# Scan stage and last two stages of a four-layer kernel: one program per engine, chunks overlapped, blocks in fixed slots

## The reference, cut to what matters

```python
# stage 4: gated linear scan over all 2048 tokens; its input is a layernorm, then an RMS norm
xn = x / max(norm(x), 1e-12) * sqrt(128) * gamma
q, kv, a = split(xn @ W_qkva.T); a = sigmoid(a)
h[t] = a[t] * h[t-1] + kv[t]                    # per feature
out = q * h
# stages 7 and 8: dense feed-forward, 128 -> 512 -> 128 (the first with its own layernorm gain and shift)
x = x + relu(x2 @ w1 + b1) @ w2 + b2
x = x + relu(layernorm(x) @ W1 + b1) @ W2 + b2
```

## Time and profile before

| | |
|---|---|
| three runs | 942.45, 938.83, 939.75 us; median 939.75 |
| profiled execution | 939.33 us, span 937.5 us |
| TensorE busy | 749.5 us, 80% of the span |
| VectorE busy | 694.7 us, 74% |
| ScalarE busy | 553.9 us, 59% |
| GpSimd busy | 429.6 us, 46% |
| mean granted TensorE clock | 0.891 of full speed |

### The profile page before, as it was taken

The page is one execution under the profiler, slowest core; times in us unless marked ns, Lnnn a source line. Parts: engine busy times, 40 slices in busy tenths (PEclk is TensorE's granted clock), DMA queues, the critical chain, the costliest instruction groups (busy, mean ns, idle before and its releaser), DMA issues. The chain is left out here.

```text
span 937.5 us, 10990 instructions
## 1 busy us (share of the span) xinstructions
PE 749.5 (80%) x3306; PEld 474.2 (51%) x3306; DVE 694.7 (74%) x1644; ACT 553.9 (59%) x877; POOL 429.6 (46%) x463
## 2 busy tenths in 40 slices
PE   4788996898988799886579888868677867767776
PEld 3566763454655577764456665633232222224554
DVE  6686875989896377776766667778888778784675
ACT  5254664746745356543136666768799887784333
POOL 6547655454442045556426766624433123303554
PEclk9998999979877689999769999978899888898799
DMA  4100000001000000001000000000000000000001
GB/s 137 58 12 15 23 15 25 23 16 31 23 8 11 1 1 1 0 1 34 1 0 1 1 1 0 1 0 1 1 1 0 1 1 0 1 1 0 1 0 46
DMA packets 9610, 11.59 MB, mean 12 GB/s; under 512 B 720, under 2 KB 5712, under 8 KB 9552
## 3 DMA queue, kind: packets, MB, share of 16 engines
q1 hardware_dynamic: 9552, 10.89, 4.0%
HBM read 9.84 MB, written 1.05 MB: 12 GB/s over the span
## 5 line engine op out<-in xcount | busy, mean ns | idle before, releaser
L949 POOL TENSOR_TENSOR rbuf<-B,rbuf 128x512 fp32r<-128x512 f32 x154 | 200.6, 1305 | 175.6 <-ACT rbuf L872 111.2
L917 DVE TENSOR_TENSOR B<-B,spread_bank 128x512 f32<-128x512 f32 x128 | 87.1, 682 | 45.2 <-ACT B L864 35.2
L872 ACT ACTIVATE rbuf<-B 128x512 fp32r<-128x512 f32 x132 | 82.9, 628 | 41.5 <-PE y_bank L697 32.4
L695 PE MATMUL y_bank<-rbuf,WH 128*128 128x512 f32 x174 | 75.5, 434 | 29.8 <-POOL rbuf L949 18.8
L864 ACT ACTIVATE B<-gate_banks,WR 128x512 f32<-128x512 f32 x96 | 66.0, 688 | 39.1 <-PE gate_banks L697 29.0
L904 DVE TENSOR_TENSOR B<-B,up_banks 128x512 f32<-128x512 f32 x68 | 46.5, 684 | 49.0 <-PE up_banks L697 30.1
L861 ACT ACTIVATE B<-gate_banks 128x512 f32<-128x512 f32 x68 | 40.8, 599 | 64.6 <-PE gate_banks L697 63.5
L695 PE MATMUL gate_banks<-XH,WH 128*128 128x512 f32 x168 | 75.5, 450 | 2.5 <-ACT YT L1273 0.8
L477 POOL TENSOR_SCALAR small<-small 128x4 f32<-128x4 f32 x36 | 7.5, 209 | 141.0 <-DVE small L378 140.4
L697 PE MATMUL y_bank<-rbuf,WL 128*128 128x512 f32 x174 | 70.2, 404 | 0.0
L696 PE MATMUL y_bank<-rbuf,WH 128*128 128x512 f32 x174 | 70.2, 404 | 0.0
(11 more groups left out here) (290 smaller groups left out, 2060.3 us busy)
## 6 DMA issues: line engine op xcount, KB each, us to landing
STG<-in_w_split SPq DMA_DIRECT2D x27, 256.0 KB, 2.7
X<-in_x SPq DMA_DIRECT2D x4, 256.0 KB, 6.0
out<-X SPq DMA_DIRECT2D x4, 256.0 KB, 2.3
WR<-in_w_raw SPq DMA_DIRECT2D x1, 524.5 KB, 5.5
STG<-in_w_exact SPq DMA_DIRECT2D x2, 256.0 KB, 2.7
STG<-in_w_split SPq DMA_DIRECT2D x5, 64.0 KB, 1.9
STG<-in_w_split SPq DMA_DIRECT2D x1, 192.0 KB, 2.3
STG<-in_w_split SPq DMA_DIRECT2D x1, 128.0 KB, 2.1
```

The costliest lines, as they stand in the source:

```text
L695: nc.tensor.matmul(dst, w[0], x[0], start=start, stop=False)
L872: nc.scalar.activation(rbuf[n % 2][:, :], HO[n % 3], ACT.Copy).then_inc(hh_ready, 1)
L917: nc.vector.tensor_tensor(HO[n % 3], src, SP[:, :], ALU.mult).then_inc(h_ready, 1)
L949: e_.tensor_tensor(rbuf[2 + n % 2][:, :], AO[n % 2] if f.dense else HO[n % 3], rbuf[n % 2][:, :].bitcast(F32), ALU.subtract).then_inc(hl_r ...
```

## The change

- The scan stage is played once, when chunk 0 is reached, as one written-out list per engine (`gated_pe`, `gated_act`, `gated_dve`, `gated_pool`), with two sets of SIG, HS and YS. The carry is read from the other HS. Chunk 0's products stand on TensorE in expert stage 3, ahead of its last two down projections; its sigmoid stands on ScalarE ahead of that stage's result copy, behind a one-element sigmoid that brings the table.
- Three fronts (stage 4 chunks 2 and 3, stage 5 chunk 0; ON_ACT) are normalised on ScalarE, with a scale and a bias from GpSimd, turned into bank R in place of TN, and XH comes from ScalarE too.
- Stage 4's norm takes one power of 128 x variance in place of two.
- The last group of weight pieces may no longer be done in the scan stage, only from expert stage 5 on.
- Expert stages 1 and 5 project block 1 ahead of the first routing weights.
- The dense stages become eight slots of four blocks with four buffers of each kind (`ring_*`). ScalarE writes both the high part and the relu from the bank; the subtraction is on VectorE, and for the fourth block of slots 0 to 5 on GpSimd; the down projection lags three blocks. A slot ends with one front and one tail. The first two projections stand in the last step of stage 6.

```diff
+        ON_ACT = ((4, 2), (4, 3), (5, 0))
+        def norm_bank(n, c):
+            return R if count(n, c) >= count(7, 2) or (n, c) in ON_ACT else TN
...
+                if n == 4:
+                    chain(nc.gpsimd.tensor_scalar(ve[:, :], mv[:, :, 1], float(P), 1e-24 * EPS, ALU.mult, ALU.max))
...
+            if pos == 1 and on_act:
+                a.wait_ge(rstd_ready, m + 1)
+                a.wait_ge(norm_turned, m)
+                for j in range(TL):
+                    i = nc.scalar.activation(XN[:, j, :], X[:, c * TL + j, :], ACT.Identity, scale=rs[:, j:j + 1],
+                                             bias=nb[:, j:j + 1])
...
                 for at_ in lagged(f, c, b, f.lag):
                     down(*at_)
+                    if f is FFN1 and at_ == (NC - 1, f.blocks - 3):
+                        scan_pe(pe, 0)
...
+            if c >= 2:
+                a.wait_ge(yt_ready, count(4, c - 1))
             a.wait_ge(scan_in, 3 * c + 1)
-            nc.scalar.activation(buf[c % 2], SB[c % 2][0][:, :], ACT.Sigmoid).then_inc(sig_ready, 1)
+            nc.scalar.activation(SIG[c % 2], SB[c % 2][0][:, :], ACT.Sigmoid).then_inc(sig_ready, 1)
...
+        def gated_pe(pe):
+            tail_pe(pe, 3, 3)
+            scan_pe(pe, 1)
+            tail_pe(pe, 4, 0)
+            front_pe(pe, 4, 2, 2)
+            scan_pe(pe, 2)
+            front_pe(pe, 4, 3, 2)
+            tail_pe(pe, 4, 1)
+            front_pe(pe, 5, 0, 2)
+            scan_pe(pe, 3)
+            tail_pe(pe, 4, 2)
+            front_pe(pe, 5, 0, 4)
+        def gated_act(a):
+            scan_act(a, 1)
+            front_act(a, None, 4, 2, 1)
+            front_act(a, None, 4, 2, 2)
+            front_act(a, None, 4, 3, 1)
+            scan_act(a, 2)
+            front_act(a, None, 4, 3, 2)
+            front_act(a, None, 5, 0, 1)
+            front_act(a, None, 5, 0, 2)
+            scan_act(a, 3)
+            nc.scalar.activation(junk[:, 1:2], zero, ACT.Exp)
+            front_act(a, None, 5, 0, 6)
+        def gated_dve(v, chain):
+            front_dve(v, chain, 4, 2, 0)
+            scan_dve(v, chain, 0)
+            scan_out(v, 0)
+            tail_dve(v, chain, 3, 3)
+            front_dve(v, chain, 4, 3, 0)
+            tail_dve(v, chain, 4, 0)
+            scan_dve(v, chain, 1)
+            front_dve(v, chain, 4, 2, 3)
+            scan_out(v, 1)
+            front_dve(v, chain, 5, 0, 0)
+            scan_dve(v, chain, 2)
+            tail_dve(v, chain, 4, 1)
+            front_dve(v, chain, 4, 3, 3)
+            scan_out(v, 2)
+            front_dve(v, chain, 5, 1, 0)
+            front_dve(v, chain, 5, 0, 3)
+            scan_dve(v, chain, 3)
+            front_dve(v, chain, 5, 0, 5)
+            tail_dve(v, chain, 4, 2)
+            scan_out(v, 3)
+            for pos in (7, 8, 9):
+                front_dve(v, chain, 5, 0, pos)
+            front_dve(v, chain, 5, 1, 1)
...
+        def ring_pe(pe, j):
+            for b in range(RB4):
+                k = RB4 * j + b
+                if k >= 2:
+                    ring_up(pe, k)
+                if k == 3:
+                    project_pe(pe, NC - 1)
+                if k >= 3:
+                    ring_down(pe, k - 3)
+            if ring_front(j):
+                front_pe(pe, *ring_front(j), 2)
+            tail_pe(pe, *ring_tail(j))
...
+        def ring_act(a, j):
...
+            for b in range(RB4):
...
+                nc.scalar.activation(HID[n % DEEP], UPD[n % DEEP][:, :], ACT.Relu, bias=bias).then_inc(hh_ready, 1)
...
+                nc.scalar.activation(AOD[n % DEEP], UPD[n % DEEP][:, :], ACT.Relu, bias=bias).then_inc(act_done, 1)
+                if b == 0 and j:
+                    if ring_front(j - 1):
+                        front_act(a, None, *ring_front(j - 1), 2)
+                if b == 2:
+                    if j:
+                        result(j - 1)
...
+        def ring_dve(v, chain, j):
+            front, last = ring_front(j), ring_front(j - 1) if j else None
+            for b in range(RB4):
+                if not ring_low_on_pool(RB4 * j + b):
+                    ring_low(nc.vector, v, RB4 * j + b)
+                if b == 0 and front:
+                    front_dve(v, chain, *front, 0)
+                if b == 1:
+                    if last:
+                        front_dve(v, chain, *last, 3)
+                    if front:
+                        front_dve(v, chain, *front, 1)
+            tail_dve(v, chain, *ring_tail(j))
...
-                limit = {"stage0": 0, FFN0: 1, "attn": 2, FFN1: 2, "scan": 3, FFN2: 3}.get(body, 3)
+                limit = {"stage0": 0, FFN0: 1, "attn": 2, FFN1: 2, "scan": 2, FFN2: 3}.get(body, 3)
```

More of the change, by code:

```diff
@@ L1433, in build, with gated_pool @@
+        def gated_pool(g, chain):
+            for n, c in ((4, 2), (4, 3), (5, 0), (5, 1)):
+                front_pool(g, chain, n, c, 0)
         UL = 16
@@ new lines, in ring_tail, with ring_low_on_pool, ring_up @@
+        def ring_tail(j):
+            return divmod(count(6, NC - 1) + j, NC)
+        def ring_low_on_pool(k):
+            return k % RB4 == 3 and k // RB4 < SLOTS - 2
+        def ring_up(pe, k):
+            j, b = divmod(k, RB4)
+            f, c = ring_of(j)
+            n = FFN3.block0 + k
+            if b == 0:
+                pe.wait_ge(piece_ready, READY_AT[f.up])
+                pe.wait_ge(piece_ready, READY_AT[f.down])
+                pe.wait_ge(xl_ready, count(f.norm, c) + 1)
+            if k < DEEP:
+                pe.wait_ge(r_ready, PALL - 1 + k // 2)
+            else:
+                pe.wait_ge(act_done, n - DEEP + 1)
+            mm3(UPD[n % DEEP][:, :], wh(f.up, b * P), (chunk(XH, c, PAD), chunk(XL, c, PAD)), True, True)\
+                .then_inc(first_full, 1)
@@ new lines, in ring_down @@
+        def ring_down(pe, k):
+            j, b = divmod(k, RB4)
+            f, c = ring_of(j)
+            n = FFN3.block0 + k
+            if b == 0:
+                if j == 0:
+                    pe.wait_ge(oq_read, NC - 1)
+                else:
+                    pe.wait_ge(yt_ready, count(f.tail, c) - (1 if j > 1 else 0))
+            pe.wait_ge(hl_ready, n + 1)
+            mm3(YD[j % 2][:, :], wh(f.down, b * P), (HID[n % DEEP], LOD[n % DEEP]), b == 0, b == RB4 - 1)\
+                .then_inc(down_done, 1)
@@ L1796, in build @@
         HOOKED = ("attn", "keys", "queries")
+        RINGS = ("ring3", "ring4")
         def walk(which, eng, chain, do_front, do_tail):
-            late = False
             for body, c, tail, norm, route in slots():
-                was_late, late = late, body == "scan" or isinstance(body, Ffn) and body.dense
-                late_norm = norm if not late else route if was_late else None
+                if body in RINGS:
+                    j = c + NC * RINGS.index(body)
+                    ring_dve(eng, chain, j) if which == 2 else (ring_pe, ring_act)[which](eng, j)
+                    continue
+                if body == "scan":
+                    if c == 0:
+                        gated_dve(eng, chain) if which == 2 else (gated_pe, gated_act)[which](eng)
+                    continue
                 def hook(pos):
@@ L1818, in hook @@
                     else:
[L1819 removed]
+                        front = norm if pos in NORM_STEPS else route
                         if front:
@@ L1824, in walk @@
                 else:
-                    first = () if body != "scan" else (3, 0) if which == 2 else (2,)
-                    for pos in first:
-                        hook(pos)
                     args = [c, hook]
@@ L1901, in _ @@
                     attn_pool(g, chain, c, hook, lambda: work(limit))
+                elif body == "scan":
+                    if c == 0:
+                        gated_pool(g, chain)
                 else:
```

225 lines of the change are left out of this document (152 added, 73 removed), and 1 row of the table STEPS_AT.

## The result

The changed kernel takes 899.8 us (median of 4 runs, 897.5 to 900.9) against 939.3 for the kernel before on the same chip: ratio 0.958, 95% interval 0.956 to 0.960. The prediction was 907, in 8 of 10 cases 896 to 922. So it was faster as forecast, and by 7 us more than forecast. The profiled execution took 897.48 us for a span of 895.7; against the profiled one of before that is 41.8 us less.

What follows compares the result with a forecast made beforehand. TensorE bounds the expert stage, no engine the serial scan stage; the last two stages lie between. Terms -15.5 - 3 - 1 + 4 - 17 = -32.5 from 939.33 give 906.8, say 907 us; 8 in 10: 896 to 922.

Steps and rivals of the forecast that it cites:

- Scan stage: Stretch between two expert stages: overlapping its serial rounds was to save 15.5 us, bounds -19 and -7.
- named as late next: Scan stage: from chunk 2's norm on, ScalarE was expected to be the engine running late, chunk 3's tile normalised at 442.65.
- 1 us on slow matmuls as a lump: Scan stage: a third of the dozen matmul groups on the path at the lower clock takes 1 us back.
- One power: Norms in the expert stage in front: one power for two, 1.5 us for each of two chunks, -3, bounds 0 and -4.2.
- Early block: Start of the next expert stage: block 1 projected before the routing weights come, -1 us, bounds 0 and -2.
- Pieces: Seven weight pieces move from scan stage to next expert stage: 0.6 us each, +4, bounds 0 and +13.3.
- Last two stages: Ring of slots, 8.1 us each, set by the order of VectorE's program: -17 us, bounds -21 and -8.
- The 3 us that I gave back for the lower clock: Last two stages: -20.2 us at full clock, cut to -17 for 10 us of time at the lower clock.
- The first rival: Last two stages: GpSimd's subtraction and power slow VectorE, slots 1.0 to 1.5 us longer, half the gain, 915 us; chance 0.20.
- a piece 0.81 and not 1.9: Rival, next expert stage: each weight piece costs its full 1.9 us, +9, 916 us; chance 0.10.
- the scan stage gained 15.0 and not 7: Rival: scan stage stays serial as programs wait in order, gaining 7 us instead of 15.5, 916 us; chance 0.06.
- the clock in the slots rose: Rival, last two stages: TensorE drops to 1.2 GHz for the whole ring, 937 us or slower; chance 0.04.

## Why the prediction was right, step by step

- **Scan stage: -15.5 forecast, -15.0 measured** (the gap), of it 2.0 from its own shorter power and 13.0 from the programs. The result copy slips 1.03 us, forecast 0.9. Counted from the last weighing of stage 3, the steps came within 0.4 us of the forecast up to chunk 3's normalised tile (12.7 us behind it, forecast 12.55). Its low part then came 1.6 us late, and so did everything behind it. ScalarE, which was named as late next, isn't what cost this: chunk 2's matmuls ran at 1.2 GHz up to 435.89 (pitch 0.43 us) and ended about 1.4 us later than at 2.4 GHz, and chunk 3's transposes stand behind them. The forecast had put 1 us on slow matmuls as a lump, so the sum is near for a reason that it named, but the engine to shorten next was wrong. No run has the scan stage's programs alone: the 13.0 is what is left when one power is taken out, and what each overlap in it gives stays open.
- **One power: -3 forecast, -5.8 measured.** This is the step that failed. The mechanism was right (low parts owed meanwhile), the term mis-sized, and outside its bounds of 0 to -4.2: I took 1.5 for each of two chunks. Each gives the whole 2.2 of the chain, none of it hidden, and the second 1.45 more, since TensorE no longer waits 3.16 us and no longer runs its next ten matmuls at 1.2 GHz. I had the row of that wait and didn't look at the pitch behind it.
- **Early block: -1 forecast; 0.6 to 1.9 in one trace.** Together with the pieces stage 5 got 4.8 longer, forecast 3. **Pieces: +4 forecast, +5.7 measured** (0.81 each for 0.6). The waits for GpSimd came out as named, 4.2 us more, forecast 4 in all.
- **Last two stages: -17 forecast, -20.8 measured** (-20.3 alone; about 2 us more against the slower of the two traces of the old stages). Slot 8.06 us for 8.1, last down group 62.3 us behind the readout for 61 to 65. The 3 us that I gave back for the lower clock weren't due: TensorE, busy 53.5 of 63.5 us, was granted 0.97 where it had 0.90, with a single spell at 1.2 GHz in the whole stretch. So the full-clock sum of -20.2 was the right one. The first rival (slots of 9 to 9.6) fell for the reason given: GpSimd's subtraction starts 0.77 us after the normalisation is over (859.81 and 859.04) and meets the sum that reads a bank.
- Three normalisation groups stand on ScalarE, not the four that I named: I misread a list of three.
- The sum of the parts is -36.8 for my -32.5. With 939.3 as the start this makes 902.5; the last 3 us to 899.8 lie within what one execution differs by. The two large misses (2.8 and 3.8 us) go the same way, so the time came near the low end of the range and not by errors that cancel. The rivals fall by the same stretches: the slots took 8.06 us, a piece 0.81 and not 1.9, the scan stage gained 15.0 and not 7, and the clock in the slots rose.

## What to carry to other kernels

When a chain of small instructions on GpSimd is cut, price what its end releases as well: the whole wait of the engine behind it, and the clock that TensorE may keep when it waits less. In a ring of slots, first show by adding work to the suspect engine whether its busy time or its order sets the period (0.69 us more cost nothing here), then reorder, and count what comes from the period and what from the first slot; and when the order no longer binds, look at which instruction the other engine's work stretches, and move that work to stand beside one that it doesn't. Where the clock makes 1% from run to run, cut the traces at equal instructions and compare stretches.

## What the runs showed of the hardware

- Beside GpSimd's 128x512 subtraction (1.29 us): a VectorE sum of two SBUF tiles takes 1.38 us for 0.70, four normalisations of 128 columns up to 3.0 for 1.11, and a copy of one SBUF tile 1.41 for 0.48 (kernel before, 404.57 and 430.10); a sum that reads a bank (0.68) and the statistics (0.88) are not stretched. A step of 128x32 took 1.07 for 0.19 beside a weight piece.
- A switch of ScalarE's table cost its 1.28 us load and nothing else: the load ends at 424.43 and the next function starts at 424.44. The Trainium skill (ScalarE: Activation LUTs, section "What ACT_TABLE_LOAD costs") adds a drain to each switch; no gap of that kind is in this trace either.
- TensorE fell to 1.2 GHz behind a wait of 3.16 us and not behind one of 2.17 or 0.98 in the same expert stage. The length of the wait alone doesn't decide: in the scan stage of the changed kernel it ran at 1.2 GHz behind a wait of 2.23 us (433.20) and at 2.4 behind one of 2.45 (440.21), and the same 3.05 us wait ahead of the second slot was followed by a spell at 1.2 GHz (from 835.5) in the changed kernel and by none in the version with the normalisations on VectorE. In the other slots, with 1.4 us of idle time in each, it kept 2.4 GHz; in the attention stage it was granted 0.77 or 0.84, by execution, with the same code.
